# Reordering a time-mixing stage so that the next chunk's first steps run between the current chunk's scans

## The reference

```python
xs = jnp.pad(x, ((0, 0), (1, 0), (0, 0)))[:, :-1]      # the token before
xx = xs - x
xxx = x + xx * time_maa_x                              # "first mix"
m = jnp.tanh(xxx @ time_maa_w1).reshape(Bc, Tc, 5, TM_DIM)
m = jnp.einsum('btfe,fec->fbtc', m, time_maa_w2)       # low-rank product, 5 parts
xw = x + xx * (time_maa_w + mw)                        # and xk, xv, xr, xg alike
r = xr @ W_r;  k = xk @ W_k;  v = xv @ W_v
g = jax.nn.silu(xg @ W_g)
w = time_decay + jnp.tanh(xw @ time_decay_w1) @ time_decay_w2
wdec = exp(-exp(w))
# per head (16 heads of 8): y_t = r_t (S + u k_t v_t^T);  S = S * wdec_t + k_t v_t^T
# then group norm per head, * ln_gamma + ln_beta, and
return yn * g @ W_o
```

## Time and profile before

| what | value |
|---|---|
| median of 3 runs | 2998.38 us (2984.62 to 2999.5) |
| the profiled execution | 2976.21 us, span 2974.1 us, mean granted PE clock 0.905 |
| the time-mixing stage in it | about 2549 to 2929 us of the span |
| busy over the span | PE 78%, DVE 69%, ACT 49%, POOL 31% |

### The profile page before, as it was taken

One profiled execution on the slowest core, in us unless ns is written; L12 is line 12 of the kernel. 1 busy time (PEld: TensorE's weight loads), 2 busy tenths in 40 slices (PEclk: granted clock), 3 DMA queues, 4 the chain that ended last, 5 costly groups with the idle time before them and its releaser, 6 DMA issues. The chain is left out here.

```text
span 2974.1 us, 45405 instructions
## 1 busy us (share of the span) xinstructions
PE 2325.8 (78%) x13880; PEld 1443.8 (49%) x13880; DVE 2038.1 (69%) x5199; ACT 1464.5 (49%) x3130; POOL 933.3 (31%) x978
## 2 busy tenths in 40 slices
PE   3498689849877799999999986769685996777776
PEld 3397577739844122222222224559564884222224
DVE  4466788846554799999999944556676665676774
ACT  2265311126544388888888872236532664233232
POOL 5644234444433200010100002544446443121321
PEclk9999799969988699999999997879796997899998
DMA  4122100012221300000000001012301222000000
GB/s 153 46 64 71 41 8 15 15 30 65 65 65 36 134 20 18 20 18 19 17 19 18 15 1 39 31 49 66 91 21 44 64 62 84 0 0 0 0 0 29
DMA packets 111194, 115.75 MB, mean 39 GB/s; under 512 B 21904, under 2 KB 94192, under 8 KB 110192
## 3 DMA queue, kind: packets, MB, share of 16 engines
q1 hardware_dynamic: 92512, 76.38, 8.8%
q0 software_dynamic: 17408, 35.95, 3.6%
q10 hardware_dynamic: 1040, 0.53, 0.1%
HBM read 67.55 MB, written 44.83 MB: 38 GB/s over the span
## 5 line engine op out<-in xcount | busy, mean ns | idle before, releaser
L1878 DVE TENSOR_REDUCE attn_mx<-bank 128x1 f32<-128x512 f32 x1024 | 641.3, 683 | 62.9 <-PE bank L1657 55.0
L1779 ACT ACTIVATE attn_pT<-bank 128x512 f32<-128x512 f32 x1024 | 540.1, 603 | 127.6 <-PE bank L1672 127.1
L1657 PE MATMUL bank<-attn_K,attn_Q 48*128 48x512 bf16 x1024 | 336.7, 397 | 50.4 <-DVE attn_mx L1878 28.9
L1672 PE MATMUL bank<-attn_Q,attn_K 51*128 51x512 bf16 x1024 | 331.6, 387 | 2.2 <-ACT attn_pT L1779 1.6
L1685 PE MATMUL bank<-attn_pT,attn_vb 128*32 128x512 f32 x2048 | 277.1, 612 | 20.3 <-ACT attn_pT L1779 12.1
L1838 POOL TENSOR_TENSOR attn_m_rem<-attn_m_rem,attn_m_parts 8x128 f32<-8x128 f32 x128 | 53.4, 417 | 679.9 <-ACT attn_m_parts L1792 679.9
L1657 PEld LDWEIGHTS bank<-attn_K,attn_Q 48*128 48x128 bf16 x1024 | 72.0, 94 | 377.0 <-DVE attn_mx L1878 324.8
L2585 POOL TENSOR_TENSOR mix_rS<-mix_rT,mix_S 128x512 f32<-128x512 f32 x64 | 81.6, 1279 | 264.8 <-ACT mix_gT L2566 205.2
L1004 PE MATMUL bank<-mix_prod_qk,ident 128*128 128x256 f32 x512 | 121.6, 393 | 0.0
L1004 PEld LDWEIGHTS bank<-mix_prod_qk,ident 128*128 128x128 f32 x512 | 101.3, 199 | 25.2 <-issue 11.8
L2519 PE MATMUL bank<-mix_rS,mix_sel 128*128 128x512 f32 x128 | 75.4, 678 | 41.6 <-POOL mix_rS L2585 41.6
(11 more groups left out here) (619 smaller groups left out, 5898.0 us busy)
## 6 DMA issues: line engine op xcount, KB each, us to landing
w<-in_L_w SPq DMA_DIRECT2D x4, 2048.0 KB
ffn0a_x_ring<-xs_rows SPq DMA_DIRECT2D x72, 65.0 KB, 1.8
ffn0b_x_ring<-xs_rows SPq DMA_DIRECT2D x72, 65.0 KB
ffn2a_x_ring<-xs_rows SPq DMA_DIRECT2D x72, 65.0 KB, 1.8
ffn2b_x_ring<-xs_rows SPq DMA_DIRECT2D x72, 65.0 KB, 1.8
ffn0a_y_back<-y_rows SPq DMA_DIRECT2D x8, 512.0 KB, 3.8
ffn1a_in_y_back<-y_rows SPq DMA_DIRECT2D x8, 512.0 KB
ffn2a_y_back<-y_rows SPq DMA_DIRECT2D x8, 512.0 KB, 3.8
```

Source lines behind the costliest of these rows:

```text
L1657: nc.tensor.matmul(a_bank[n % 3][:], slot(net.Q, h, 0, KROWS)[:, qt * P:(qt + 1) * P], slot(net.K, h, 0, KROWS)[:, hf * CH:(hf + 1) * CH], ...
L1672: nc.tensor.matmul(s_bank[n % 3][:], slot(net.K, h, 0, KROWS + MROWS)[:, kt * P:(kt + 1) * P], slot(net.Q, h, 0, KROWS + MROWS)[:, hf * CH ...
L1779: nc.scalar.activation(pT[:, kt % RING, hf * CH:(hf + 1) * CH], s_bank[(n * HPB + hf) % 3][:], ACT.Exp, scale=HD ** -0.5).then_inc(exp_rea ...
L1878: nc.vector.tensor_reduce(mx[:, h % 2, qt, hf:hf + 1], a_bank[n % 3][:], AX.X, ALU.max).then_inc(a_used, 1)
```

## The change

Only `time_mix_stage` and two small helpers change. The arithmetic is the same.

- VectorE no longer copies tokens: the first mix and the mixed inputs read `xnT` directly (at the beginning of a sequence with one extra instruction of one column). A dummy instruction of one column after `mix_rku` is gone too.
- The next chunk's first mix stands after scan 1, PE's hidden product after read 2, its corrections w and k after read 4 and v after read 5, in banks that are free by then. Its mixed inputs still come after the last scan.
- After the last scan come the mixes w, k, v, r, g, and between them the bonus and the whole y of the chunk that ended. On PE the decay path is first, then k, the first spread of v, the centering, r, the second spread, v, variance, g. `mix_rku` is made after scan 0, `group` after scan 2, `add` and the statistics after scan 4, the norm's `shift` after scan 6.
- The bonus sums and the projection stand after reads 1 and 3; the projection goes into bank 6 instead of the y bank. `gT` is double-buffered.
- ScalarE loads its function tables by hand, two loads per chunk where three were.
- After the last chunk the same steps of the group norm run as before, with the table for the logarithm already loaded.

The diff, cut to its core:

```diff
-        xs = part.sb("xs", [P, 2, CH + 1])
...
+        w_bank, out_bank, y_bank = net.bank[1], net.bank[6], net.bank[7]
+        MIX_BANK = {W: g_bank, K: k_bank, V: v_bank, R: r_bank, G: g_bank}
...
+            def mix(c, f):
+                pe.wait_ge(m_kept, 2 * c + (1 if f in (W, K) else 2))
+                if f == W:
+                    need(pe, g_kept, c)
+                if f == R:
+                    need(pe, bonus_made, c)
+                if f == G:
+                    pe.wait_ge(mixed, NMIX * c + 1)
+                lhs, rhs = (w2a[:, f, :], m0[:]) if f < 4 else (w2b[:], m1[:])
+                nc.tensor.matmul(MIX_BANK[f][:], lhs, rhs, start=True, stop=True).then_inc(mix_ready, 1)
...
+            for c in range(NCH):
+                last = c - 1
+                decay_hidden(c)
+                mix(c, R)
+                mix(c, G)
+                decay(c)
+                linear(c, "k", K, k_bank, k_ready)
+                repeat(c, 0)
+                if c > 0:
+                    center(last)
+                linear(c, "r", R, r_bank, r_ready)
+                repeat(c, 1)
+                linear(c, "v", V, v_bank, v_ready)
+                if c > 0:
+                    variance(last)
+                linear(c, "g", G, g_bank, g_ready)
                 for j in range(HD):
                     if j + 2 < HD:
+                        repeat(c, j + 2)
+                    if j == HD - 1 and c > 0:
+                        norm.turn(pe, last)
+                    read_state(c, j)
+                    if j == 1:
+                        bonus_sums(c)
+                    if j == 2 and c + 1 < NCH:
+                        hidden(c + 1)
+                    if j == 3 and c > 0:
+                        project(last)
+                    if j == 4 and c + 1 < NCH:
+                        mix(c + 1, W)
+                        mix(c + 1, K)
+                    if j == 5 and c + 1 < NCH:
+                        mix(c + 1, V)
+            c = NCH - 1
+            center(c)
+            variance(c)
+            project(c)
+            norm.turn(pe, c)
...
+            nc.scalar.preload_act_table_set("silu_and_others")
+            squash(0)
+            for c in range(NCH):
+                last = c - 1
+                squash_decay(c)
+                nc.scalar.preload_act_table_set("natural_log_exp_and_others")
+                decay(c)
+                need(act, scanned, scans(c, 0))
+                keep(c, kT, k_bank, k_ready, k_kept)
+                if c > 0:
+                    squares(last)
+                need(act, rs_ready, scans(c, 0))
+                keep(c, rT, r_bank, r_ready, r_kept)
+                need(act, bonus_made, c)
+                keep(c, vT, v_bank, v_ready, v_kept)
+                if c > 0:
+                    deviation(last)
+                nc.scalar.preload_act_table_set("silu_and_others")
+                gate(c)
+                if c + 1 < NCH:
+                    squash(c + 1)
+                if c > 0:
+                    norm.keep(act, last)
+            c = NCH - 1
+            nc.scalar.preload_act_table_set("natural_log_exp_and_others")
+            squares(c)
+            deviation(c)
+            norm.keep(act, c)
...
+                    if j == 5 and c > 0:
...
+            def first_mix(c):
+                begins = c % HPB == 0
+                cur = tokens(c)
+                if begins:
+                    chain.then(nc.vector.tensor_scalar(xx[:, 0:1], cur[:, 0:1], -1.0, None, ALU.mult))
+                    chain.then(nc.vector.tensor_tensor(xx[:, 1:CH], cur[:, 0:CH - 1], cur[:, 1:CH], ALU.subtract))
+                else:
+                    chain.then(nc.vector.tensor_tensor(xx[:], src[:, c * CH - 1:(c + 1) * CH - 1], cur, ALU.subtract))
+                need(dve, m_ready, 2 * c)
                 chain.wait()
+                nc.vector.scalar_tensor_tensor(x3[:], xx[:], vec["maa_x"], cur, ALU.mult, ALU.add).then_inc(x3_ready, 1)
+
+            def mix(c, f):
+                dve.wait_ge(mix_ready, NMIX * c + f + 1)
+                chain.then(nc.vector.scalar_tensor_tensor(corr[:, f % 2, :], MIX_BANK[f][:], vecs[:, 5 + f:6 + f], xx[:],
+                                                          ALU.add, ALU.mult))
+                if f == W:
+                    need(dve, g_ready, c)
                 chain.wait()
+                nc.vector.tensor_tensor(xm[:, f, :], corr[:, f % 2, :], tokens(c), ALU.add).then_inc(mixed, 1)
...
+            def group(c):
+                dve.wait_ge(yc_kept, c + 1)
+                dve.wait_ge(rstd_ready, c + 1)
+                chain.then(nc.vector.tensor_tensor(yn[:], yc[:], rstd[:], ALU.mult))
+                chain.wait()
+                chain.then(nc.vector.tensor_scalar(yn[:], yn[:], vec["ln_gamma"], vec["ln_beta"], ALU.mult, ALU.add))
+                dve.wait_ge(g_kept, c + 1)
+                chain.wait()
+                need(dve, out_ready, c)
+                nc.vector.tensor_tensor(yg[:], yn[:], gT[:, c % 2, :], ALU.mult).then_inc(yg_ready, 1)
...
+            first_mix(0)
+            for c in range(NCH):
+                last = c - 1
+                mix(c, W)
+                if c > 0:
+                    add_bonus(last)
+                mix(c, K)
+                if c > 0:
+                    whole(last)
+                mix(c, V)
+                mix(c, R)
+                mix(c, G)
+                begin_state(c)
                 for j in range(HD):
+                    step(c, j)
                     if j == 0:
+                        bonus_terms(c)
+                    if j == 1 and c + 1 < NCH:
+                        first_mix(c + 1)
+                    if j == 2 and c > 0:
+                        group(last)
+                    if j == 4 and c > 0:
+                        add(last)
+                        stats(last)
+                    if j == 6 and c > 0:
+                        norm.apply(dve, last)
+            c = NCH - 1
+            add_bonus(c)
+            whole(c)
+            group(c)
+            add(c)
+            stats(c)
+            norm.apply(dve, c)
...
```

More of the change, by code:

```diff
@@ new lines, in decay_hidden, with decay, linear @@
+            def decay_hidden(c):
+                pe.wait_ge(mixed, NMIX * c + W + 1)
+                need(pe, kv_done, scans(c, 0))
+                nc.tensor.matmul(w_bank[0:TD, :], dw1[:], xm[:, W, :], start=True, stop=True).then_inc(w1_ready, 1)
+            def decay(c):
+                pe.wait_ge(w1_kept, c + 1)
+                nc.tensor.matmul(w_bank[:], dw2[:], tw[:], start=True, stop=True).then_inc(w2_ready, 1)
+            def linear(c, k, f, bank, ready):
+                pe.wait_ge(mixed, NMIX * c + f + 1)
+                nc.tensor.matmul(bank[:], W_[k][:], xm[:, f, :], start=True, stop=True).then_inc(ready, 1)
@@ new lines, in repeat, with bonus_sums @@
+            def repeat(c, j):
+                if j == 0:
+                    pe.wait_ge(mixed, NMIX * c + V + 1)
+                    need(pe, kv_done, scans(c, 0))
+                if j == 1:
+                    pe.wait_ge(e1_ready, c + 1)
+                if j > 1:
+                    pe.wait_ge(kv_done, scans(c, j - 1))
+                nc.tensor.matmul(rep_bank[j % 2][:], Wv_rep[:, j, :], xm[:, V, :], start=True, stop=True).then_inc(rep_ready, 1)
+            def bonus_sums(c):
+                pe.wait_ge(r_kept, c + 1)
+                pe.wait_ge(rku_ready, c + 1)
+                nc.tensor.matmul(r_bank[:], W_["blockones"][:], rku[:], start=True, stop=True).then_inc(bonus_ready, 1)
@@ L2459, in center, with read_state @@
+            def read_state(c, j):
+                if j == 0:
+                    need(pe, sq_ready, c)
+                pe.wait_ge(rs_ready, scans(c, j) + 1)
+                nc.tensor.matmul(y_bank[:], sel[:, j, :], rs[:, j % 4, :], start=(j == 0), stop=(j == HD - 1)).then_inc(y_acc, 1)
             def center(c):
@@ new lines, in _ @@
+            hidden(0)
+            for f in (W, K, V):
+                mix(0, f)
+            for c in range(NCH):
[14 more added lines that the diff above has]
+                linear(c, "g", G, g_bank, g_ready)
@@ L2513, in body @@
                 for j in range(HD):
                     if j + 2 < HD:
-                        repeat(j + 2)
-                    if j == 0:
-                        need(pe, out_added, c)
-                    pe.wait_ge(rs_ready, HD * c + j + 1)
-                    nc.tensor.matmul(y_bank[:], sel[:, j, :], rs[:, j % 4, :],
-                                     start=(j == 0), stop=(j == HD - 1)).then_inc(y_acc, 1)
-                if not is_first(c):
-                    norm.turn(pe, c - 1)
@@ L2654, in body @@
-                dve.wait_ge(lin_kept, 4 * c + 3)
-                dve.wait_ge(bonus_ready, c + 1)
-                chain.then(nc.vector.tensor_tensor(bonus[:], vT[:], net.bank[3][:], ALU.mult))
-                dve.wait_ge(y_acc, HD * (c + 1))
-                chain.wait()
```

(5 more changed lines are left out.)

237 lines of the change are left out of this document (86 added, 151 removed).

## The result

| | before | after |
|---|---|---|
| median (range, runs) | 2995.14 us (2984.62 to 2999.5, 4) | 2913.64 us (2907.47 to 2918.48, 4) |
| profiled execution, its span | 2976.21, 2974.1 us | 2907.47, 2905.7 us |
| the stage in it, first instruction to last copy's end | 380.9 us | 304.7 us |
| steady chunk | 45.7 us | 35.9 us |

A forecast was written before the change was run, and what follows sets the result against it. The stage was taken as bound by VectorE's chain with its waits on PE and ScalarE. Savings of 62.4 + 12.7 + 3.9 + 1.4 = 80.4 us, put on the median 2998.4, gave 2918 us, range 2893 to 2952.

The forecast's parts named there:

- The period: Steady chunk of the stage: 33.1 VectorE work + 1.2 + 0.3 + 0.7 = 35.3 us, 10.4 less than 45.7.
- scans beside GpSimd: Scans 4, 6 and 7 still directly follow a GpSimd product and are delayed 0.45 us each, 1.35 per chunk.
- first mix, tensor-scalar: Second instruction of the first mix behind scan 1 waits 0.85 us for GpSimd; group's tensor-scalar behind scan 2, 0.75.
- `mix_rku`: VectorE's instruction behind scan 0: no delay by GpSimd, 0 us.
- wait of the `add`: VectorE waits 1.2 us per chunk for PE's projection, behind product 3 and read 3; bounds 0 to 2.5.
- PE's clock: Lower clock hits PE's matmuls at places without slack: 0.7 us per chunk, between 0 and 7.
- Chunk 0: PE's and ScalarE's work runs beside the mixes, so the end of scan 7 comes 3.9 us earlier.
- The tail: After the last chunk the second ScalarE table load goes and shortens the path: 1.4 us.
- B: Rival: displaced GpSimd delays and the clock cost nothing; period 32.6 us, saves 99 us, time 2899 us; chance 0.12.
- C: Rival: PE bounds each chunk's head, eight matmuls at half speed; period 41.5 us, time 2964 us; chance 0.10.
- D: Rival: denser PE held at the lower clock all through the stage; 36 us slower, 3034 us; chance 0.03.
- E: Rival: an overlooked semaphore keeps the old order; only copy and table load won, about 6 us, 2992 us; chance 0.03.

The follow-up runs named there:

- experiment 1: Changed kernel with the next chunk's first mix, hidden product and corrections put back behind the last scan, plus small moves: 2941.9 us, 0.9816 of the kernel before.
- experiment 2: Changed kernel with the last chunk's group norm, projection and add put ahead of scan 0: 2953.4 us, 0.9847 of the kernel before.
- experiment 3: Changed kernel with the decay path last on PE and ScalarE, spreads 0 and 1 behind it: 2939.6 us, 0.9813 of the kernel before.
- experiment 6: Changed kernel with the bonus terms (mix_rku) behind scan 4 and the bonus sums behind read 5: 2910.1 us, 0.9711 of the kernel before.
- experiment 7: Changed kernel with bonus terms behind scan 4 and mix_kv for scans 2 and 3 between the instructions of first mix and group: 2901.3 us, 0.9679 of the kernel before.
- experiment 8: As experiment 7, with the bonus product between w's correction and mixed input, and PE's g product behind spread 2: 2901.3 us, 0.9672 of the kernel before.
- experiment 4: Changed kernel with GpSimd multiplying only 8 of the 512 columns of each state product: 2878.4 us, 0.9609 of the kernel before.
- experiment 5: Changed kernel with PE products made twice, in two kernels: k and r 2936.4 us (0.9798 of the kernel before), v and g 2913.0 us (0.9746).

## Why the prediction was right, step by step

**The mechanism** was the one forecast: VectorE is busy for 94% of a chunk, and the serial paths of one chunk lie beside the scans of the other (experiments 1 to 3 show each part, 6 to 8 that work taken off VectorE shortens the period). That 2918 came within 4.4 us of 2913.6 is partly luck, since the same kernel gave 2925.6 in the second comparison; what was forecast is the stage, 80.4 us shorter, and it came 76.2 us shorter.

**The period**, 35.3 forecast, 35.9 measured. Its terms, measured in the chunk of the timeline above:

| term | forecast | measured |
|---|---|---|
| scans beside GpSimd | 1.35 | 0.60 + 0.42 + 0.35 = 1.37 |
| first mix, tensor-scalar | 0.85, 0.75 | 0.65, 0.65 |
| first mixed input | 0.4 | 0.5 to 0.8 |
| `mix_rku` | 0 | 1.13 |
| wait of the `add` | 1.2 | 1.03 |
| spread 0, `mix_rku`'s wait | 0.3 | 0.29 |
| PE's clock | 0.7 | 0 |

The mis-sized terms are two, and by luck they nearly cancel. "`mix_rku` behind scan 0: 0" was wrong: I saw that VectorE comes there when ScalarE's copy of r is done, and did not ask who else waits for that copy. GpSimd's product 0 does. Both are released within 0.04 us, GpSimd has its turn first, and `mix_rku` ends 0.55 us after it, 1.13 us late. Experiment 6 takes this away, and 1.5 us go. The clock term was wrong the other way: PE, busy 31.7 of 36.1 us, is granted 1.00 in the steady chunks. What I had feared for the changed kernel happens in some chunks when one of its parts is undone (experiments 1 and 2).

The `add`'s wait came as worked out from the earlier trace rows: scan 3 ends at 2652.61, the `add` starts 3.52 us later (3.5 forecast), through product 3 (1.27), read 3 and the projection (1.05). It is a path of its own: when experiments 4, 6 and 8 shorten VectorE's work, this wait or one for a spread takes back a part.

**The sum.** Chunk 0, from its first instruction to the end of scan 7, went from 38.5 to 35.9 us: 2.6 instead of 3.9. Its first scan came at 15.3 us after the start and not at 14.6, after a wait of 0.8 for spread 0, and waits of 0.6 and 0.8 for later spreads followed. Chunks 1 to 6, from there to the end of scan 7 of chunk 6, went from 275.3 to 215.2: 60.1 instead of 62.4. Chunk 7, from there to the end of the last y, went from 49.2 to 37.4: 11.8 instead of 12.7. The tail, from the last y to the last copy, went from 18.0 to 16.2: 1.8 instead of 1.4. Together 76.2 instead of 80.4 us.

In the tail the exponential starts 0.77 us after the logarithm, and before it could start only 2.05 us after it, when the second load of the earlier trace rows ended: the load was worth its own 1.28 us. By the Trainium skill ("ScalarE: Activation LUTs", section "What ACT_TABLE_LOAD costs") the table switch would have been worth 2.66 us, and the trace doesn't bear this out here. Most of the remaining 0.5 is the centering on PE, 1.12 us instead of 1.50.

That the median moved by 81.5 us, and 69.5 in the second comparison, around these 76, fits the scatter of the program outside the stage. The choice to put the gain on the median of the runs mattered more than the error of any term: put on the profiled execution, the forecast would have been 2895.8. A moving time outside the stage was one of the stated signs of being wrong. In the profiled executions it was 7.8 us longer after, but the medians show no such shift.

**The rivals.** B (delays and clock cost nothing, 2899) had the clock right and the delays wrong: the displaced ones, with `mix_rku`, cost 2.9 to 3.2 us per chunk (the table), of 4.5 for all the sharing (experiment 4). C, PE as the bound of the head, was half right: the head has no slack (experiment 5), but it is not at half clock. D and E are excluded, by the clock of 1.00 and by the waits that are gone. How much of the 9.8 us per chunk comes from PE's clock having risen from 0.93 to 1.00 was not separated.

**Still open.** It was not tried whether a shorter PE head would bring 8 to its forecast of 32.4, nor what decides whether PE's clock falls in a chunk of experiments 1 and 2.

## What to carry to other kernels

Where an engine waits on serial paths, place the next tile's first steps and the last tile's final steps among its long independent instructions, and price each part with the others in place: undone one by one they cost more than the whole brought. Before you place an instruction beside another engine, ask what releases that engine too; put instructions that it doesn't delay (here those that read PSUM) into its turn. When the first engine is 94% busy, look at the second (here PE, 88%), since the next gain ends there.
